# A state-space mixer with experts on one core: decay products moved to GpSimd, silu and sums to VectorE, diagonal products at full width

## The reference

```python
zxbcdt = hidden_states @ in_proj_w.T              # gate, xBC, dt
xBC = silu(depthwise_conv4(xBC) + conv_b)         # x: 128 heads of 64; B, C: 8 groups of 128
dt = softplus(dt + dt_bias); Adt = -exp(A_log) * dt; xs = x * dt
A_cumsum = cumsum(Adt)                            # within a chunk
L = exp(segment_sum(Adt))                         # decay from token j to token i, j <= i
Gm = einsum('bcihn,bcjhn->bhcij', C, B)           # scores
Y_diag = einsum('bhcij,bcjhd->bcihd', Gm * L, xs)
states = ...                                      # per chunk, carried with exp of the chunk sums
Y_off = einsum('bckhn,bchdn,bhck->bckhd', C, states, exp(A_cumsum))
y = (Y_diag + Y_off + D * x) * silu(gate)
y = rmsnorm_per_group(y) * norm_w
out = y @ out_proj_w.T
```

## Time and profile before

| | |
|---|---|
| median of 3 runs | 2345.82 us (2335.52 to 2347.23) |
| the profiled execution | 2340.48 us, span 2338.4 us, 39600 instructions |
| mean granted clock of TensorE | 0.966 |
| PE busy | 2096.4 us (90%) |
| DVE busy | 1585.1 us (68%) |
| ACT busy | 1231.7 us (53%) |
| POOL busy | 1152.2 us (49%) |

### The profile page before, as it was taken

How to read it: one execution, slowest core, us unless ns; L and a number is a source line. 1 busy time by engine, 2 the same in 40 slices (tenths; PEclk the granted TensorE clock), 3 DMA queues, 4 the chain that set the end, 5 groups by cost and what they waited for, 6 DMA issues and landing times.

```text
span 2338.4 us, 39600 instructions
## 1 busy us (share of the span) xinstructions
PE 2096.4 (90%) x11776; PEld 1731.7 (74%) x11776; DVE 1585.1 (68%) x2766; ACT 1231.7 (53%) x2680; POOL 1152.2 (49%) x987
## 2 busy tenths in 40 slices
PE   3889998989999989999998899899989888989897
PEld 2678777877777777777787778777777767767775
DVE  5797489739973996498659956984698463167314
ACT  2676367627762775377437744864476323522341
POOL 0377247814781578157716661765277414330332
PEclk7999999999999999999999999999999999999999
DMA  2343034203421342044113412331243027941894
GB/s 69 123 127 90 19 100 131 73 29 104 128 63 37 111 130 64 24 118 134 48 49 109 128 37 70 104 113 37 71 115 101 19 100 279 404 140 44 283 392 150
DMA packets 143765, 261.22 MB, mean 112 GB/s; under 512 B 19521, under 2 KB 35905, under 8 KB 143553
## 3 DMA queue, kind: packets, MB, share of 16 engines
q1 hardware_dynamic: 134848, 231.35, 31.2%
q0 software_dynamic: 7520, 24.65, 3.3%
q10 hardware_dynamic: 1184, 2.62, 0.3%
HBM read 233.38 MB, written 25.17 MB: 111 GB/s over the span
## 4 chain that ended last, share of the span: by engine, by line
PE 40%; issue 25%; POOL 21%; DVE 11%; ACT 1%; another core or an unknown queue 1%; POOLq 0%; DMA 0%; DVEq 0%; SPq 0%; ACTq 0%
PE bank L1475 25%; PE bank L1758 5%; POOL gt L681 5%; POOL Y L692 5%; POOL cv L699 4%; POOL Y L675 3%; PE bank L1608 3%; POOL wl L659 2%; PE bank L1770 2%; PE bank L1622 1%; DVE mem L1226 1%; POOL mem L650 1%; DVE Y L1184 1%; PE bank L1745 1%; DVE mem L1152 1%
## 5 line engine op out<-in xcount | busy, mean ns | idle before, releaser
L1475 PE MATMUL bank<-xh,wh 128*128 128x512 f32 x1288 | 522.2, 405 | 17.2 <-POOL wl L659 10.3
L1475 PE MATMUL bank<-xh,wl 128*128 128x512 f32 x1288 | 504.1, 391 | 0.0
L1475 PE MATMUL bank<-xl,wh 128*128 128x512 f32 x1288 | 503.5, 391 | 0.0
L659 POOL TENSOR_TENSOR wl<-raw,wh 128x512 fp32r<-128x512 f32 x144 | 183.9, 1282 | 511.1 <-ACT wh L857 510.5
L1184 DVE SCALAR_TENSOR_TENSOR Y<-bank,cpar,Y 128x511 f32<-128x511 f32 (+2 forms) x384 | 287.0, 747 | 21.3 <-ACT Y L874 11.1
L1475 PE MATMUL bank<-wh,ah 128*128 128x512 f32 x576 | 241.7, 420 | 65.7 <-DVE wl L1139 24.3
L1475 PEld LDWEIGHTS bank<-xh,wh 128*128 128x128 f32 x1288 | 243.2, 189 | 65.8 <-issue 12.2
L1475 PEld LDWEIGHTS bank<-xh,wl 128*128 128x128 f32 x1288 | 242.6, 188 | 52.6
L1475 PEld LDWEIGHTS bank<-xl,wh 128*128 128x128 f32 x1288 | 243.5, 189 | 45.1 <-issue 0.5
L1249 DVE TENSOR_TENSOR al<-Y,ah 128x512 fp32r<-128x512 f32 x128 | 108.8, 856 | 201.0 <-ACT ah L937 201.0
L650 POOL TENSOR_TENSOR mem<-mem,hpt 128x384 f32<-128x384 f32 x128 | 106.7, 834 | 275.9 <-DVE mem L1152 259.3
(11 more groups left out here) (211 smaller groups left out, 4228.7 us busy)
## 6 DMA issues: line engine op xcount, KB each, us to landing
mem<-c_rows SPq DMA_DIRECT2D x176, 256.0 KB, 3.6
mem<-wffn_d SPq DMA_DIRECT2D x62, 512.0 KB
E<-c_rows SPq DMA_DIRECT2D x256, 96.0 KB, 2.8
raw<-wconv_d SPq DMA_DIRECT2D x80, 256.0 KB, 2.8
cv<-c_rows SPq DMA_DIRECT2D x80, 256.0 KB, 3.6
raw<-wgate_d SPq DMA_DIRECT2D x64, 256.0 KB, 2.7
raw<-wout_d SPq DMA_DIRECT2D x64, 256.0 KB, 2.6
slots_y<-quad SPq DMA_DIRECT2D x62, 256.0 KB
```

Source lines behind the costliest of these rows:

```text
L659: inc(pool.tensor_tensor(wl[:, W_SLOT[p], :], raw[:, R_SLOT[p], :], wh[:, W_SLOT[p], :], ALU.subtract), w_lo)
L1475: got = mm(out, l, r, start=first and n == 0, stop=last and n == 2)
```

## The change

- The products of decay and scores go from DVE to POOL, between L650's successor and the remainder.
- Silu of all 20 convs is done by DVE in one instruction each (`STT` with gt and the tile); POOL's two instructions for each of the last 11 go.
- The running sums of squares (14 in a group) go from POOL to DVE.
- E holds exponentials from the start: the preparation takes exp of all c once and writes a second table `e_rows`; SP fetches E from it, ACT's exponential of E goes, and DVE waits for the fetch before the off scaling.
- `xs` gets 64 zero columns between the two heads of a chunk. The diagonal product uses 128 columns of it, head 0 followed by zeros, or zeros followed by head 1, and adds both heads up in one result of 128 partitions; chunk is now the outer loop. Number and moving size of the products stay.
- The zeros need room: `spare` becomes a tile of its own, and the squares `sq` move into the tile of B, so the next group's first conv waits for the sums.

```diff
+        spare = sb("spare", [P, 2 * HID])
+        XW = 3 * HD
+        xsp = [v.rearrange("p (c n) -> p c n", c=CH)
+               for v in (mem[:, 0:CH * XW], mem[:, CH * XW:2 * CH * XW], spare[:, 0:CH * XW])]
+
+        def xs_heads(u, chunks):
+            return xsp[u % 3][:, 0:chunks, :].rearrange("p c (z d) -> p c z d", d=HD)[:, :, 0:3:2, :]
...
-        sq = sb("sq", [P, 2, SEQ])
+        sq = quad[:, 0, :].rearrange("p (n s) -> p n s", n=2)
...
-                        sp.dma_start(E[h * HD:(h + 1) * HD, u % ER, :], c_rows[i, a:a + 1, b * SEQ + P:(b + 1) * SEQ]
+                        sp.dma_start(E[h * HD:(h + 1) * HD, u % ER, :], e_rows[i, a:a + 1, b * SEQ + P:(b + 1) * SEQ]
...
+            for v in xsp:
+                step(pool.memset(v[:, :, HD:2 * HD], 0.0))
...
+                    u = k - A_ - 1
+                    if 0 <= u < UNITS:
+                        pair, b = unit(u)
+                        for h in range(2):
+                            n = 2 * u + h
+                            now(pool, decay_ok, i, n + 1)
+                            if n == 0:
+                                now(pool, g_ok, i, 2)
+                            inc(pool.tensor_tensor(L[n % LR], L[n % LR],
+                                    G[:, b * CH:(b + 1) * CH, :].rearrange("p c i -> p (c i)"),
+                                    ALU.mult), lg_ok)
...
-                    kc = k - 1
-                    if EARLY <= kc < NCONV:
-                        now(pool, conv_th, i, kc + 1)
-                        dst = piece(*conv_unit(kc))
-                        inc(pool.tensor_tensor(gt[:, kc % 2, :], dst, gt[:, kc % 2, :], ALU.mult), conv_vt)
-                        now(pool, conv_vt, i, kc - EARLY + 1)
-                        inc(pool.tensor_tensor(dst, dst, gt[:, kc % 2, :], ALU.add), conv_late)
...
-                        inc(pool.tensor_tensor(acc[:, n % 2, :], acc[:, n % 2, :], sq[:, n % 2, :], ALU.add), ss_add)
...
+            n = step(nc.scalar.activation(v_hm, c_hm, ACT.Exp))
+            act.wait_ge(act_step, n)
+            act.dma_start(e_rows.rearrange("g h n -> (g h) n"), v_hm).then_inc(scr_rows, 16)
...
-                        e_arrived(act, i, u)
-                        inc(nc.scalar.activation(E[:, u % ER, :], E[:, u % ER, :], ACT.Exp), e_ok)
...
                         if tile == 0:
                             before(act, tr_mm, i, 4)
+                            before(act, ss_add, i, NGATE - BATCH)
...
-                        inc(TTn(xs[:, u % 3, :, :].rearrange("p c (h d) -> p c h d", d=HD),
+                        inc(TTn(xs_heads(u, CH),
...
-                    if 0 <= kc < EARLY:
+                    if 0 <= kc < NCONV:
...
-                        inc(STT(dst, gt[:, kc % 2, :], 1.0, dst, ALU.add, ALU.mult), conv_early)
+                        inc(STT(dst, gt[:, kc % 2, :], 1.0, dst, ALU.add, ALU.mult), conv_ok)
...
-                        now(dve, e_ok, i, u + 1)
+                        e_arrived(dve, i, u)
...
-                            now(dve, decay_ok, i, n + 1)
-                            if n == 0:
-                                now(dve, g_ok, i, 2)
-                            inc(TTn(L[n % LR], L[n % LR],
-                                    G[:, b * CH:(b + 1) * CH, :].rearrange("p c i -> p (c i)"),
-                                    ALU.mult), lg_ok)
...
+                    n = k - 3 - NCONV
+                    if BATCH <= n < NGATE:
+                        now(dve, sq_ok, i, n + 1)
+                        if n >= 2 * BATCH:
+                            now(dve, ss_add, i, n - 2 * BATCH + 1)
+                        inc(TTn(acc[:, n % 2, :], acc[:, n % 2, :], sq[:, n % 2, :], ALU.add), ss_add)
...
-                        for h in range(2):
-                            for c in range(CH):
-                                hs = slice(h * HD, (h + 1) * HD)
-                                last = mm(b4(DG[u % 2])[hs, c, :], xs[:, u % 3, c, hs],
-                                          L[(2 * u + h) % LR][:, c * P:(c + 1) * P], start=True, stop=True)
+                        for c in range(CH):
+                            for h in range(2):
+                                last = mm(b4(DG[u % 2])[:, c, :], xsp[u % 3][:, c, h * HD:h * HD + P],
+                                          L[(2 * u + h) % LR][:, c * P:(c + 1) * P], start=h == 0, stop=h == 1)
```

More of the change, by code:

```diff
@@ L170, in hybrid_layer @@
         c_rows = nc.dram_tensor("c_rows", (GROUPS, GH, TOK), f32, kind="Internal").ap()
+        e_rows = nc.dram_tensor("e_rows", (GROUPS, GH, TOK), f32, kind="Internal").ap()
         xn_dram = nc.dram_tensor("xn_dram", (TOK, HID), f32, kind="Internal").ap()
@@ L207, in hybrid_layer @@
         conv_th = counted("conv_th", NCONV)
-        EARLY = 9
-        conv_early = counted("conv_early", EARLY)
-        conv_vt = counted("conv_vt", NCONV - EARLY)
-        conv_late = counted("conv_late", NCONV - EARLY)
+        conv_ok = counted("conv_ok", NCONV)
         tr_mm = counted("tr_mm", 2 + 2 + UNITS)
@@ L216, in hybrid_layer @@
         dcol_ok = counted("dcol_ok", 2)
-        e_ok = counted("e_ok", UNITS)
         fall_ok = counted("fall_ok", 2 * UNITS)
@@ L378, in conv_done @@
         def conv_done(eng, i, n):
-            if n <= EARLY:
-                now(eng, conv_early, i, n)
-            else:
-                now(eng, conv_late, i, n - EARLY)
+            now(eng, conv_ok, i, n)
         T_B, T_G, T_X, A_, B_, C_, D_ = 4, 6, 8, 9, 10, 11, 11
@@ L419, in hybrid_layer @@
         PH_PREP, PH_MIXER = 1, 2
-        PREP = dict(dt=13, scan=16, tokc=18, diff=20, tables=20, decay=9, cend=11)
+        PREP = dict(dt=13, scan=16, tokc=18, diff=20, tables=20, decay=10, cend=12)
         FFN_ORDER = [("gu", 0, 0), ("gu", 1, 0), ("gu", 0, 1), ("dn", None, 0), ("gu", 1, 1), ("dn", None, 1)]
@@ L501, in _ @@
                             hp_in, 16)
-                        sp.wait_ge(scr_rows, 16)
+                        sp.wait_ge(scr_rows, 32)
                         sp.wait_ge(phase, 4 * PH_PREP)
@@ L591, in _ @@
         def _(pool):
-            credit(pool, (w_lo, g_ok, conv_vt, conv_late, xd_ok, y_ok, y_gated, ss_add, f_lo))
+            credit(pool, (w_lo, g_ok, lg_ok, xd_ok, y_ok, y_gated, f_lo))
             steps = [0]
@@ L692, in _ @@
                         inc(pool.tensor_tensor(dst, dst, gt[:, n % 2, :], ALU.mult), y_gated)
-                    n = k - 3 - NCONV
-                    if BATCH <= n < NGATE:
-                        now(pool, sq_ok, i, n + 1)
-                        if n >= 2 * BATCH:
-                            now(pool, ss_add, i, n - 2 * BATCH + 1)
-                        inc(pool.tensor_tensor(acc[:, n % 2, :], acc[:, n % 2, :], sq[:, n % 2, :], ALU.add), ss_add)
             phase_end(pool, PH_MIXER)
@@ L755, in _ @@
         def _(act):
-            credit(act, (w_hi, tap0, conv_th, tr_act, g_act, fall_ok, decay_ok, e_ok, gate_th, sq_ok,
+            credit(act, (w_hi, tap0, conv_th, tr_act, g_act, fall_ok, decay_ok, gate_th, sq_ok,
                          nrm_sd, y_hi, f_hi, f_th, a_hi))
@@ L865, in _ @@
                         if k == 4:
-                            act.wait_ge(scr_rows, 16)
+                            act.wait_ge(scr_rows, 32)
                             act.wait_ge(scr_heads, 16)
@@ L1022, in _ @@
         def _(dve):
-            credit(dve, (wo_lo, taps, conv_early, lg_ok, xs_ok, s_step, s_ok, off_ok, ydiag_ok, gate_ok, dcol_ok,
+            credit(dve, (wo_lo, ss_add, taps, conv_ok, xs_ok, s_step, s_ok, off_ok, ydiag_ok, gate_ok, dcol_ok,
                          nrm_ok, y_lo, res_ok, f_hg, f_h, a_lo, dn_acc))
@@ L1213, in _ @@
                         now(dve, off_mm, i, u + 1)
-                        now(dve, e_ok, i, u + 1)
+                        e_arrived(dve, i, u)
                         inc(STT(E[:, u % ER, :], bank[OF][:, 0:(CH - 1) * P], 0.5, E[:, u % ER, :], ALU.mult,
                                 ALU.mult), off_ok)
-                    u = k - A_ - 1
-                    if 0 <= u < UNITS:
-                        pair, b = unit(u)
-                        for h in range(2):
-                            n = 2 * u + h
-                            now(dve, decay_ok, i, n + 1)
-                            if n == 0:
-                                now(dve, g_ok, i, 2)
-                            inc(TTn(L[n % LR], L[n % LR],
-                                    G[:, b * CH:(b + 1) * CH, :].rearrange("p c i -> p (c i)"),
-                                    ALU.mult), lg_ok)
                     if NCONV <= k < NCONV + NGATE:
```

4 lines of the change are left out of this document (1 added, 3 removed).

## The result

| | before | after |
|---|---|---|
| median | 2344.95 us (2335.52 to 2351.67, 12 runs) | 2354.47 us (2346.49 to 2362.83, 12 runs) |
| span of the profiled execution | 2338.4 us | 2344.4 us |
| mean granted clock | 0.966 | 0.964 |

The changed kernel takes 1.0043 of the time before, 95% interval 1.0028 to 1.0058: slightly slower, where I had forecast 0.8% less (2327). The time lies in my range. In the changed kernel the lines are: xs product L1153, POOL's decay products L665, remainder L672, xd L651, sum L688, gate L697; silu L1194 and taps L1185 on DVE; ACT's differences L900, exponentials L847, tap 0 L875; SP's weights L463, rows L473, E row L484.

A forecast was written before the change was run, and what follows sets the result against it. DVE was taken to bound the conv steps and a two-step ring the gate steps. Terms −0.6 − 2.5 + 1.0 + 1.1 − 1.3 = −2.3 us a group, −18 for eight, gave 2327 us under the median; range 2280 to 2358.

The forecast's parts named there:

- What bounds the kernel before: No engine alone; DVE's work binds conv steps at 7.13 us each, a two-step ring binds gate steps at 6.97.
- a ring through POOL, SP and ACT: POOL's sum, SP's row fetch, ACT, DVE, POOL: before, 13.94 us over two gate steps; changed, 20.5 over three conv steps.
- Part 1, steps 9 to 11: In step 10 DVE loses an L1226 pair (1.2) and gains one silu (about 0.6): −0.6 us a group.
- Part 2, conv steps: Steps 11 to 20: the ring sets 6.85 us a step against 7.13, −2.5 a group; ends 6.4 and 7.4 a step.
- my own two signs for the slower case: In the changed profile: POOL's products take more than 1.4 us each, or the silu more than 1.2.
- Part 3, gate steps: Steps 20 to 23: the ring grows to 15.2 us, 7.6 a step; 22.8 against 21.8, +1.0 a group.
- Part 4, wide products: Steps 23 to 26, bound by PE's own work: four unit products at +0.28 us each, +1.1 a group.
- the rival of the weight loads: Weight loads set the wide products' pace: PE 6.9 us a step, 3.4 in steps 23 to 26; 2346 us, chance 0.07.
- Part 5: End of the gate stretch: sums move to DVE, its last remainder comes earlier, PE's 3.0 us wait shrinks: −1.3 a group.
- Part 6, at nothing: ACT's removed exponentials on E, DVE's wait for E, the preparation's extra exponential, squares in BT and memsets: counted as nothing.
- POOL's sum comes late: Conv and gate steps: lock waits of 2.5 us in three steps, +3.2 a group, 2371 us; chance of slower 0.18.
- PE alone: Rival: the ring has more slack, conv steps at 6.4 us, −9.4 a group, 2271; chance 0.18, part way included.

The follow-up runs named there:

- the first and fifth experiments: Changed kernel with SP's decay rows ahead of its E row: 2296.49 us, 0.9802; with them ahead of the weight fetch too: 2266.08 us, 0.9696.
- the silu in PSUM: DVE's silu multiplies with the unconvolved PSUM product, values differ: on the changed kernel 2341.91 us, 0.9998; with decay rows ahead of weight fetch and E row 2265.57 us, 0.9694.
- narrow products: Diagonal products as 128x64 pieces again: on the changed kernel 2351.02 us, 1.0048; with decay rows ahead of weight fetch and E row 2271.22 us, 0.9694.
- the experiment on the kernel before: Kernel before, with SP's decay rows ahead of its E row, ACT's exponential of E still in each step: 2439.26 us, 1.0440.
- the rows on top: Changed kernel, with SP sending each step's decay rows ahead of both its weight fetch and its E row: 2266.08 us, 0.9696.
- POOL's early sum: Changed kernel, with POOL's sum ahead of its two decay products: 2358.95 us, 1.0071; with decay rows also ahead of weight fetch and E row: 2263.63 us, 0.9692.

## Why the prediction was wrong

*What bounds the kernel before.* Right for the conv steps: DVE's list (64.1 us also with the exponential gone and the rows early). Wrong for the gate steps: I read a ring through POOL, SP and ACT where a loop of DVE and PE binds. The ring I had traced closes in the same time, but ACT waited only 0.39 us in it, which should have told me that it was barely taut.

*Part 1, steps 9 to 11.* Right: −0.60.

*Part 2, conv steps.* Here the forecast failed, in the terms and not in the mechanism. That SP's fetch behind POOL becomes the bound is shown by the first and fifth experiments: moving the rows alone took 3.1 and then 4.8 us out of steps 11 to 20, and 2.4 and then 3.5% (56 and 81 us) out of the time. I had named only the wait for the sum; the weight fetch ahead of it, which waits for the remainder, is a link that I had not seen. Mis-sized were the lock waits (0.8 in three steps; 1.20 in the three traced, 1.45 by the silu in PSUM), and the step from the row's issue to ACT (no term for the second head's row: 0.64 in the three steps traced, and 0.19 of landing). In the mean, three steps take 21.8 where I had 20.5, and my own text had named 21.4 as the point from which it turns slower. The gain of 2.5 hung on a difference of 0.9 between two sums of which one had a term bounded only between 0 and 2.5. Of my own two signs for the slower case one came, barely: the silu took 1.22 in the mean (my mark was 1.2), POOL's products 1.28 (my mark was 1.4).
By the rule of the Trainium skill (SBUF — State Buffer, section "SBUF: two separate sides") that I quoted, a DVE instruction with two SBUF inputs takes the lock; the 1221 ns with two and 679 with one agree.

*Part 3, gate steps.* The size was right (22.6 against 22.8) for the changed kernel, where the ring does bind: 19.53 and 17.60 once it is loosened. What I compared it with was misread, and the change of +0.88 came near my +1.0 because the two loops of the kernel before happen to close in the same time: that is luck. With the rows early in both, these steps gain 3.8 us from the swap (21.43 against 17.60).

*Part 4, wide products.* The diagonal records take 1.79 from start to next (L1602 at 811.04, L1616 at 812.83), as the rows of the expert stage gave. But the steps hardly grow by it: from the diagonal products of step 23 to those of step 26 PE takes 17.09 on the average, before 16.75, so +0.34 in three steps where I had 0.28 in each. A part comes back at once: the off products behind the wide records take 0.58 (812.83 to 813.41), before 0.69.

With and without the ring, narrow products give no time that can be measured, so the rival of the weight loads falls too. By the Trainium skill (TensorE: Matmul & The Clock Gate, section "LDWEIGHTS") 16 records should have cost 0.85 more, an estimate from its price by columns, not 0.28; the rows decide.

*Part 5.* The wait for the last remainder did not shrink (22.6, before 24.3). The stretch from step 23 to the next step 9 still ended 0.73 shorter, for a reason that neither part has: the granted clock behind that wait. From the end of this wait to the end of the next one, which is 2.18 us long in both, PE does the same products, in 14.12 us before and in 12.33 in the changed kernel (timeline of PE, fourth pass of each):

```profile
927.00 0.50 PE L1475 MATMUL bank<-wh,ah 128*128 128x512 f32 x1 [3.03 <-DVE wl L1139]
...
941.12 0.47 PE L1475 MATMUL bank<-wh,ah 128*128 128x512 f32 x1 [2.18 <-DVE al L1249]
```

```profile
929.00 0.50 PE L1470 MATMUL bank<-wh,ah 128*128 128x512 f32 x1 [2.83 <-DVE wl L1140]
...
941.33 0.47 PE L1470 MATMUL bank<-wh,ah 128*128 128x512 f32 x1 [2.18 <-DVE al L1244]
```

In the first 7 us of it the granted clock was 0.76 before and 1.00 after the change. In the first seven passes it was below 1 in all seven before, and in three with the change. That the sum of parts 4 and 5 came near is luck too.

*Part 6, at nothing.* The kernel before with that exponential taken once confirms it for this term (0.9984 [0.9970, 0.9997], some 4 us). But it is not worth nothing in what it allows: the experiment on the kernel before lost 4% without it.

*The rivals.* Nearest came "POOL's sum comes late", by its lock waits between the 1.7 that decide and the 2.5 I gave it, if the second row is counted with them. PE alone, at 6.4 a step, was reached only when both the ring and the lock waits were gone (6.31, with the silu in PSUM); with the ring cut alone, the locked silu binds at 6.74. The time itself, 0.4% above, lies in the band of no visible change, to which I gave 0.26; my own chances add up to 0.28 there (0.15 + 0.07 + a third of 0.18), and 0.12 for slower.

Why a pass with the silu in PSUM loses almost what it gains can in the main be read from the trace with the rows on top (3.7 us from step 24 to the next step 9). PE waits there for this silu in the tiles of B and C, 13.3 us in 16 waits, 1.7 a pass, and rows on top alone has no such wait: the late banks. And in the 7 us behind the wait for the last remainder the granted clock was 0.76 to 0.81 in place of 1.00, which makes PE 1.5 later at its next wait. The last 0.5 is open.

Open too: how much of the changed kernel's time is the lower clock in the steps with units. From step 11 to step 23 it was granted 0.96 to 0.98 in each pass, before 0.98 to 1.00, with the rows on top 1.00; it falls behind the waits of PE, and no run separates the two.

## What to carry to other kernels

When work moves to an engine whose completion another queue waits for, follow that queue's order: everything behind the waiting transfer waits too. Here, once the rows were issued early, the swap was worth 3%, and issuing one transfer ahead of two that it does not depend on was the difference between 0.4% slower and 3% faster. A queue can have more than one such link, and cutting one may show nothing, as POOL's early sum did. Which transfer is the urgent one depends on the rest of the program: the same order lost 4% before the change. And where two sums differ by less than the range of one term, the chance of either sign should be near even.

## What the runs showed of the hardware

The same stall of PE can leave the granted clock alone or bring it down. In step 17 of the kernel before PE waits 1.99 to 2.01 us before its transposes in every pass. In the fourth pass the clock stayed where it was (columns: us, PE busy, PEclk, DMA share, GB/s):

```profile
828.00:833.80 5.80, 3.82 (x22) 1.00 0.61 165
833.80:837.00 3.20, 3.17 (x28) 1.00 0.27 97
```

In the third, after the same wait and the same 3.82 us of work ahead of it, it fell:

```profile
601.30:607.10 5.80, 3.82 (x22) 1.00 0.62 167
607.10:610.30 3.20, 3.18 (x20) 0.58 0.28 95
```

A mean of 0.58 lies between the levels of 1.2 and 2.4 GHz, near the lower. The 16 diagonal records took 1.51 us from first to next in three of the eight passes, and 2.75 to 2.82 in the other five. So my fourth pass does not stand for all eight in this row. It cost the kernel before nothing there: steps 11 to 20 took 64.16 to 64.23 in the three, and 64.11 to 64.27, once 64.89, in the five.

In the changed kernel PE waited 2.10 us before the transposes of step 16, and in the 3.8 us after it the clock was 0.57:

```profile
819.40:825.80 6.40, 4.31 (x26) 0.99 0.29 87
825.80:829.60 3.80, 3.79 (x20) 0.57 0.45 160
```

The 16 diagonal records took 3.08 us there in place of 1.95, and 3.38 after another wait of 2.25. Behind the wait for the last remainder the clock stayed after 2.83 us (the changed kernel) and 2.64 (rows on top), and fell after 3.03 (before) and 2.65 (rows on top, silu in PSUM). The length of the wait alone does not decide it.
